# First loads, function table and idle products of a mixture-of-experts and attention kernel, and the place of one split

## Chip, core and metric

The kernel runs on one core of one Trainium2 chip. The metric is the device time of one execution in microseconds; lower is better. The engines are TensorE (PE, matrix products), VectorE (DVE), ScalarE (ACT), GpSimd (POOL) and SyncE (SP), which here issues every DMA transfer. Each engine has its own instruction queue, run in order; the queues meet only at semaphores.

## What is computed

Two layers in sequence on x of 8 x 512 x 256. The first picks one of eight experts for each of the 8 batches; the second is a transformer block with 16 heads of 16, a bias of 8 x 16 x 512 x 512 (134 MB, the main traffic) and an adaptive norm fed by an embedding of a time step.

```python
# layer 0, b = one of 8 batches, its expert read from itok_B_0_7
h = gelu(x[b] @ Wi[e] + bi[e])              # 512x256 @ 256x1024
y = layernorm(h @ Wo[e] + bo[e] + x[b]) * gamma[e] + beta[e]
# layer 1
emb = silu(sin_emb(timestep)) @ W_ada + b_ada          # one row per batch
scale, shift = split(emb)
x2 = layernorm(y) * (1 + scale) + shift
q, k, v = x2 @ Wq + bq, x2 @ Wk + bk, x2 @ Wv + bv     # 16 heads of 16
p = softmax(where(mask, -inf, q @ k.T / 4 + attention_bias))
x3 = x2 + (p @ v) @ Wo + bo
out = x3 + gelu2((layernorm(x3) * g2 + beta2) @ W1 + b1) @ W2 + b2
```

## The kernel before

Three stages follow each other: the first (to about 257 us) does layer 0 and q, k, v for all 8 batches; the second is the attention; the third the rest of layer 1. Only the beginning of the first stage is touched.

**Split products.** f32 matrices are multiplied as three products of rounded halves: for a matrix a, its high half is a copy to fp32r and its low half is a minus that copy; `mm3` (L606) issues high x high, low x high and high x low. So each operand has to be split before it is used: ScalarE makes the high half (`copy`, L827), then VectorE (`low`, L1054) or GpSimd (`low`, L1375) subtracts.

**First stage, batch i.** TensorE does eight tiles `hidden(i, m)`: six products of 512 columns each (two of K by three), into one of four banks psH; tile m waits until the low half of tile m-4 is out (`v_hTl`). ScalarE's `hidden` applies Gelu in place (L864) and copies the high half hTh; VectorE's `hidden` subtracts the low half hTl from the same bank. Then TensorE does four tiles `down(i, t)`, each of eight terms m of three products of 256 columns; term m waits for the low half of hidden tile m. For batch 0 it also waits for all of the second weights wo: VectorE splits pieces 0 and 2 (`v_wo0`), GpSimd pieces 1 and 3 (`g_wol`), each behind ScalarE's copy of that piece (`a_woh`). After `down(0, 3)` comes `embedding()` (L671), which needs a chain on VectorE, ScalarE (Sin, Exp, each with a function table) and VectorE again; then the hidden tiles of batch 1.

**VectorE in batch 0.** `embedding()` is a generator of short steps on tiles of 128 x 8, each of which waits for the one before (`step`). After every low half one part of it runs: four steps (L1092 to L1095, behind the wait `d_c` for time step and frequencies), three (L1097 to L1099), four (L1101 to L1104), three (L1107 to L1109), three (L1111 to L1113), four, three, and three more, the last of which waits for the small weights (`d_w`).

**GpSimd in batch 0.** In this order: the first weights' pieces 1 and 3, `split_wo(0)` (two pieces of wo), `add_bo(0)` (writes t_xb, L1404), then for batch 1 `split_xt(1)` (t_xTl) and `split_wi(1)` (t_wil). The last two wait only for ScalarE's copies, and these for the transfers and for the eighth hidden tile of TensorE. ScalarE's order is: x of batch 0, four slices of the first weights, hidden tiles, and behind the eighth x and weights of batch 1, the embedding's three functions, the small weights.

**SyncE.** `sync_program` issues all loads by `load` (L274), in program order; a wait in it holds all that stands behind. Before, the order is: identity, expert index, x of batch 0 (transposed, t_xt), time step and frequencies; value read of the index (it needs the index load); four slices of the expert's first weights t_wi_f, its bias, second weights t_wo_f, x, three rows for the norm (broadcast); wait for the step load; small weights and biases of layer 1 (eight loads, `d_w`); seven value reads (L315); then x, rows and bias of batch 1, and t_xt, t_wi_f, t_wo_f of batch 1.

Of the kernel before, what the change touches and what calls it, by code (L numbers as in the profile page):

```python
# [11 lines left out]
ACT = mybir.ActivationFunctionType  # L12
AX = mybir.AxisListType

B, S, D, I, H, HD = 8, 512, 256, 1024, 16, 16
NT = S // 128
NK = D // 128
# [46 lines left out]
def kpn(a):  # L64
    return a.rearrange("(k p) n -> p k n", p=128)
# [46 lines left out]
def program(nc, x, x_t, itok, tstep, bias, mask, Wi, bi, Wo0, bo0, gam, bet, Wada, bada, Wq, bq, Wk, bk, Wv, bv,  # L112
            Wo, bo, W1, b1, W2, b2, g2, be2, ident, freqs, out):
    with ExitStack() as ctx:
# [23 lines left out]
        d_id, d_it, d_c, d_w, d_xt, d_wi, d_wo, d_v, d_ss, d_ssb = (sem(f"d_{n}") for n in ("id", "it", "c", "w", "xt", "wi", "wo", "v", "ss", "ssb"))  # L138
        d_wi0 = [sem(f"d_wi0{i}") for i in range(4)]
# [11 lines left out]
        v_var1, v_var2, v_var3, g_pw, g_rs1, g_rs2, g_rs3 = (sem(n) for n in ("v_var1", "v_var2", "v_var3", "g_pw", "g_rs1", "g_rs2", "g_rs3"))  # L151
# [11 lines left out]
        idf = sbuf(base, "idf", [128, 128])  # L163
        idb = sbuf(base, "idb", [128, 128], BF16)
        half = sbuf(base, "half", [128, NT])
# [3 lines left out]
        with ExitStack() as st:  # L169
            psH = [psum(st, f"psH{i}", [128, 512]) for i in range(NH)]  # L170
            psO = psum(st, "psO", [128, NT, D])
            psQ = [psum(st, f"psQ{i}", [128, 512]) for i in range(2)]
            wi_f, wo_f = sbuf(st, "wi_f", [128, NK, I]), sbuf(st, "wo_f", [128, NM, D])
# [6 lines left out]
            itk = sbuf(st, "itk", [1, B], I32)  # L180
            tsb = sbuf(st, "tsb", [128, B], I32)
            frq = sbuf(st, "frq", [128, 1])
            em = sbuf(st, "em", [128, 8, 2 * B])
# [7 lines left out]
            bqk = sbuf(st, "bqk", [128, 2, NK])  # L191
# [78 lines left out]
        def sync_program(e):  # L270
            P = Port(e)

            def load(signal, dst, src):
                e.dma_start(dst, src).then_inc(signal, 16)  # L274


            load(d_id, idf[:, :], ident)
            load(d_it, itk[:, :], itok.rearrange("(a b) -> a b", a=1))
            load(d_xt, xt[:, :, :], kpn(x_t[0]))
            load(d_c, tsb[:, :], tstep.rearrange("(a b) -> a b", a=1).broadcast_to([128, B]))  # L280
            load(d_c, frq[:, :], freqs)
            P.wait_ge(d_it, 16)
            expert = {0: e.value_load(itk[0:1, 0:1], min_val=0, max_val=7)}

            def ix(b):
                return bass.ds(expert[b], 1)

            def load_bi(b):
                load(d_bi[b % 2], bis[b % 2][:, :], bi[ix(b), :, :].rearrange("e p m -> (e p) m"))

            def load_small(b):
                for n, a in enumerate((bo0, gam, bet)):
                    load(d_s[b % 2], ob[b % 2][:, n, :], a[ix(b), :].broadcast_to([128, D]))

            def load_x(b):
                load(d_x[b % 2], xs[b % 2][:, :, :], rows(x[b]))

            for i in range(4):
                sl = slice(i * I // 4, (i + 1) * I // 4)
                load(d_wi0[i], wi_f[:, :, sl], Wi[ix(0), :, sl].rearrange("e (k p) i -> p (e k) i", p=128))  # L300
            load_bi(0)
            load(d_wo, wo_f[:, :, :], Wo0[ix(0), :, :].rearrange("e (m p) n -> p (e m) n", p=128))
            load_x(0)
            load_small(0)
            P.wait_ge(d_c, 32)
            load(d_w, wad[:, :, :], kpn(Wada))
            load(d_w, bad, bada.rearrange("(a n) -> a n", a=1).broadcast_to([B, 2 * D]))
            load(d_w, bqk[:, 0, :], bq)
            load(d_w, bqk[:, 1, :], bk)
            load(d_w, bvb[:, :], bv.rearrange("(a n) -> a n", a=1).broadcast_to([128, D]))  # L310
            load(d_w, wstage["q"][:, 0:NK, :], kpn(Wq))
            load(d_w, wstage["k"][:, 0:NK, :], kpn(Wk))
            load(d_w, wstage["v"][:, 0:NK, :], kpn(Wv))
            for b in range(1, B):
                expert[b] = e.value_load(itk[0:1, b:b + 1], min_val=0, max_val=7)  # L315
            load_x(1)
            load_small(1)
            load_bi(1)

            def next_xt(b):  # L320
                if b < B:
                    if b == 1:
                        P.wait_ge(v_xT0, 1)
                    P.wait_ge(g_xTl, b - 1)
                    load(d_xt, xt[:, :, :], kpn(x_t[b]))

            def next_wi(b):
                if b < B:
                    P.wait_ge(v_wi0, 2)
                    P.wait_ge(g_wil, b + 1)  # L330
                    load(d_wi, wi_f[:, :, :], Wi[ix(b), :, :].rearrange("e (k p) i -> p (e k) i", p=128))

            def next_wo(b):
                if b < B:
                    P.wait_ge(v_wo0, 2)
                    P.wait_ge(g_wol, b + 1)
                    load(d_wo, wo_f[:, :, :], Wo0[ix(b), :, :].rearrange("e (m p) n -> p (e m) n", p=128))

            def next_x(b):
                if b < B:  # L340
                    P.wait_ge(g_xb, b - 1)
                    load_x(b)
# [33 lines left out]
            def store_x2(b):  # L376
                P.wait_ge(v_x2, b + 1)
                load(d_x2[b % 2], sc_x2[b], x2[b % 2][:, :, :])

            next_xt(1)  # L380
            next_wi(1)
            next_wo(1)
            next_x(2)
            next_bi(2)
            next_xt(2)
# [209 lines left out]
        def tensor_program(e):  # L595
# [78 lines left out]
            def first_stage():  # L674
                for i in range(B):
                    for m in range(NM):
                        hidden(i, m)
                        if m == 3 and i >= 2:
                            turn_x2(i - 2)
                    if i >= 2:  # L680
                        drain(qkv(i - 2))
                    for t in range(NT):
                        if i == B - 1 and t == NT - 1:
                            turn_x2(B - 2)
                        down(i, t)
                    if i == 0:
                        embedding()
# [88 lines left out]
            def down2(b, t):  # L776
# [4 lines left out]
                mm3(psO2[:, t, :], [([z[:, m, ts] for z in fT], [w[:, m, :] for w in wl["2"]]) for m in range(NM)], p_dn,  # L781
                    each=[(v_fTl, 8 * b + m + 1) for m in range(NM)])

            first_stage()
            P.wait_ge(v_hTl, 8 * B)
            at = 0
# [36 lines left out]
        def scalar_program(e):  # L823
# [79 lines left out]
            def first_stage():  # L903
                split_xt(0)
                split_wi(0)
                for i in range(B):
                    for m in range(NM):
                        hidden(i, m)
                        if m == 3 and i >= 2:
                            turn_x2(i - 2)  # L910
                        if m == 0 and i == 0:
                            split_wo0()
                    steps = qkv(i - 2) if i >= 2 else iter(())
                    for n in range(7):
                        advance(steps, 1)
                        if n == 3 and i + 1 < B:
                            split_xt(i + 1)
                            split_wi(i + 1)
                    if i == 0:
                        embedding()  # L920
                        split_small()
# [74 lines left out]
            def up(b, m):  # L996
# [7 lines left out]
                P.wait_ge(p_dn, NT * b)  # L1004
                copy(fT[0][:, m, :], f[:, :], a_fTh)

            first_stage()
            for t in range(NT):
                read_mask(0, t)
# [32 lines left out]
        def vector_program(e):  # L1042
# [153 lines left out]
            def first_stage():  # L1196
                P.wait_ge(a_xTh, 1)
                low(xT[1][:, :, :], xt[:, :, :], xT[0][:, :, :], v_xT0)
                for i in (0, 2):
                    sl = slice(i * I // 4, (i + 1) * I // 4)  # L1200
                    P.wait_ge(a_wih, i + 1)
                    low(wi_s[1][:, :, sl], wi_f[:, :, sl], wi_s[0][:, :, sl], v_wi0)
                e.memset(v17[:, :, :, HD:VW], 1.0).then_inc(v_one, 1)
                for i in range(B):
                    side = norms(i - 1) if i else embedding()
                    advance(side, 1 if i else 0)
                    for m in range(NM):
                        hidden(i, m)
                        if m == 3 and i >= 2:
                            turn_x2(i - 2)  # L1210
                        if i == B - 1:
                            advance(side, SIDE_END[m])
                        else:
                            advance(side, 1 if i == 0 else SIDE_A[0] if m > 3 else 0)
                        if m == 0:
                            split_wo(i)
                    steps = qkv(i - 2) if i >= 2 else iter(())
                    for n in range(6):
                        advance(steps, 1)
                        advance(side, 3 if i else 0)  # L1220
                    advance(steps, 1)
                    for t in range(NT):
                        advance(side, SIDE_A[1] if i else t % 2)
                        if i == 0 and t == 1:
                            split_small()
                    drain(side)
# [376 lines left out]
```

## Time and profile before

| what | us |
|---|---|
| median of 3 runs (1047.84 to 1049.8) | 1048.68 |
| the profiled execution, whole | 1049.58 |
| its span in the trace | 1047.8 |
| PE busy | 989.4 (94%) |
| DVE busy | 812.4 (78%) |
| ACT busy | 772.8 (74%) |
| POOL busy | 657.5 (63%) |
| PE idle at the start, until the first low half of the weights | 8.8 |
| PE idle in the first 110 us for low halves of hidden tiles | 3.6 in 3 waits |

The busy shares are averages over three stages with different limits. A timeline row gives start and duration of an instruction, or of several alike with their count (x4). A product's record is longer than the distance to the next, since products are pipelined: the pace is read from starts. The value in brackets is the idle time of the engine just before, and what ended it.

### The profile page before, as it was taken

What the parts mean: (1) busy time and instruction counts of PE and PEld (TensorE: products, weight loads), DVE (VectorE), ACT (ScalarE), POOL (GpSimd) and SP (SyncE); (2) the same over time, 40 slices, a digit from 0 to 9 for tenths busy, and PEclk for the clock granted to TensorE, in tenths of its full rate; (3) what the DMA queues carried; (4) which work ended last, traced back from release to release, by engine and by line L of the source; (5) the groups of instructions that cost most, each with busy time, mean ns of one, the idle gap of its engine ahead of it and who ended that gap; (6) DMA issues with size and microseconds to landing.
All of it is one profiled execution on the core that took longest, in us unless ns stands there. A gap on an engine that the chain in (4) does not pass through costs nothing.

```text
span 1047.8 us, 19216 instructions
## 1 busy us (share of the span) xinstructions
PE 989.4 (94%) x6678; PEld 738.0 (70%) x6744; DVE 812.4 (78%) x1934; ACT 772.8 (74%) x1283; POOL 657.5 (63%) x349
## 2 busy tenths in 40 slices
PE   5999999999899999999998999999998799999998
PEld 4889988898565555555555555565665599888897
DVE  5599999997878988788886888888887465655563
ACT  6755576555799999899997999999998344444444
POOL 3566766763357788778976798777876654444210
PEclk9999999999999999999999999999999899999999
DMA  8748688879989999999989999999999543221001
GB/s 228 267 153 275 230 294 282 311 261 359 349 335 421 362 391 362 381 366 351 364 326 338 342 333 376 366 356 367 318 338 254 102 109 82 81 83 41 21 22 41
DMA packets 107858, 278.63 MB, mean 266 GB/s; under 512 B 13026, under 2 KB 69090, under 8 KB 87154
## 3 DMA queue, kind: packets, MB, share of 16 engines
q1 hardware_dynamic: 107762, 277.40, 75.1%
q8 instruction: 55, 0.90, 0.3%
q14 instruction: 41, 0.34, 0.1%
HBM read 222.03 MB, written 55.33 MB: 265 GB/s over the span
## 4 chain that ended last, share of the span: by engine, by line
PE 55%; ACT 21%; DMA 9%; POOL 5%; DVE 5%; issue 4%; SPq 2%; DVEq 0%; ACTq 0%; POOLq 0%
PE psO L606 15%; PE psH L606 15%; ACT t_bt L937 11%; DMA t_bt<-in_fside_Bx16xSxS 8%; PE psT L722 8%; ACT t_pt L827 6%; PE psQ L606 4%; PE psS L711 4%; PE psV L735 3%; POOL t_bt L1452 3%; PE psA L606 2%; SPq L274 2%; PE psS L709 1%; ACT t_mb L959 1%; DVE t_y L1076 1%
## 5 line engine op out<-in xcount | busy, mean ns | idle before, releaser
L1452 POOL TENSOR_TENSOR t_bt<-t_bt,t_mb 128x1024 f32<-128x1024 f32 x182 | 384.5, 2145 | 115.1 <-DMA t_bt<-in_fside_Bx16xSxS 115.1
L1254 DVE CUSTOM_DVE_ANT_0 t_bt<-psS,t_bt 128x512 f32<-128x512 f32 x512 | 338.7, 686 | 85.1 <-PE psS L711 45.7
L937 ACT ACTIVATE t_bt<-t_bt,t_nm 128x512 f32<-128x512 f32 x512 | 358.4, 737 | 19.2 <-DVE t_nm L1254 18.9
L722 PE MATMUL psT<-t_idf,t_bt 128*128 128x128 f32 x2048 | 311.3, 275 | 10.5 <-ACT t_bt L937 8.9
L722 PEld LDWEIGHTS psT<-t_idf,t_bt 128*128 128x128 f32 x2048 | 251.3, 141 | 80.0 <-ACT t_bt L937 27.8
L827 ACT ACTIVATE t_pt<-psT 128x512 f32<-128x512 f32 x317 | 192.6, 608 | 16.8 <-PE psT L722 16.6
L711 PE MATMUL psS<-t_ks,t_qs 128*128 128x512 bf16 x482 | 184.2, 382 | 13.9 <-DVE t_nm L1254 9.0
L735 PE MATMUL psV<-t_pt,t_vs 128*17 128x512 f32 x1024 | 135.0, 601 | 0.0
L1264 DVE COPY t_pt<-psT 128x512 f32<-128x512 f32 x195 | 133.7, 686 | 1.3 <-PE psT L722 1.3
L711 PEld LDWEIGHTS psS<-t_ks,t_qs 128*128 128x128 bf16 x512 | 50.0, 98 | 91.0 <-DVE t_nm L1254 70.8
L864 ACT ACTIVATE psH<-psH,t_bi 128x512 f32<-128x512 f32 x64 | 42.3, 662 | 69.2 <-PE psH L606 66.3
L1054 DVE TENSOR_TENSOR t_chTl<-t_chf,t_chTh 128x512 fp32r<-128x512 f32 x64 | 53.3, 836 | 29.7 <-ACT t_chTh L827 29.7
L606 PE MATMUL psO<-t_cw2h,t_chTh 128*128 128x256 f32 x256 | 72.9, 285 | 0.0
L606 PE MATMUL psO<-t_woh,t_hTh 128*128 128x256 f32 x256 | 72.5, 283 | 0.0
L606 PE MATMUL psO<-t_woh,t_hTl 128*128 128x256 f32 x256 | 72.5, 283 | 0.0
L606 PE MATMUL psO<-t_wol,t_hTh 128*128 128x256 f32 x256 | 72.5, 283 | 0.0
L606 PE MATMUL psO<-t_cw2h,t_chTl 128*128 128x256 f32 x256 | 72.4, 283 | 0.0
L606 PE MATMUL psO<-t_cw2l,t_chTh 128*128 128x256 f32 x256 | 72.3, 283 | 0.0
L1002 ACT ACTIVATE t_chf<-psH,t_b1c 128x512 f32<-128x512 f32 x64 | 43.7, 683 | 29.7 <-PE psH L606 27.4
L606 PE MATMUL psH<-t_xTh,t_wih 128*128 128x512 f32 x128 | 52.4, 409 | 12.7 <-DVE t_wil L1054 8.8
L827 ACT ACTIVATE t_lTh<-psX 128x512 fp32r<-128x512 f32 x16 | 8.7, 595 | 73.9 <-PE psX L759 73.9
L1375 POOL TENSOR_TENSOR t_wol<-t_wo_f,t_woh 128x2048 fp32r<-128x2048 f32 (+1 forms) x9 | 35.5, 3952 | 37.1 <-DVE t_woh L1157 34.0
(174 smaller groups left out, 1933.9 us busy)
## 6 DMA issues: line engine op xcount, KB each, us to landing
t_bt<-in_fside_Bx16xSxS SPq DMA_DIRECT2D x128, 1024.0 KB, 7.8
sc_qk<-t_parts SPq DMA_DIRECT2D x64, 384.0 KB, 6.4
t_qs<-sc_qk SPq DMA_DIRECT2D x16, 1024.0 KB, 8.0
t_ks<-sc_qk SPq DMA_DIRECT2D x16, 1024.0 KB, 10.5
t_wo_f<-in_L_cond_Wo SPq DMA_DIRECT2D x8, 1024.0 KB, 6.2
sc_qk<-t_parts SPq DMA_DIRECT2D x32, 256.0 KB, 8.4
sc_c<-t_cv SPq DMA_DIRECT2D x32, 256.0 KB
t_wi_f<-in_L_cond_Wi SPq DMA_DIRECT2D x7, 1024.0 KB, 8.7
```

Of the source, the lines that this page charges most:

```text
L606: ins = e.matmul(dst, lh[a], rh[c], start=n == 0, stop=n == last)
L711: e.matmul(s, qs[g % 2][:, h % 8, t * 128:(t + 1) * 128], ks[g % 2][:, h % 8, :], start=on_pool(u), stop=True).then_inc(p_sc, 1)
L722: ins = e.transpose(psT[turned_bank(n)][:, kk, :], bt[u % NB][:, t, kk * 128:(kk + 1) * 128], idf[:, :])
L735: ins = e.matmul(psV[32 * g:32 * g + VW, :], vs[b % 2][:, kk, u % H, :], pt[u % NP][:, kk, :], start=kk == 0, stop=kk == NT - 1)
L827: e.activation(dst, src, ACT.Copy).then_inc(signal, 1)
L864: e.activation(f[:, :], f[:, :], ACT.Gelu, bias=bis[b % 2][:, m:m + 1]).then_inc(a_gelu, 1)
L937: e.activation(p, p, ACT.Exp, bias=nm[:, n % NR:n % NR + 1], scale=-1.0).then_inc(a_exp, 1)
L1002: e.activation(f[:, :], psH2[m % 2][:, :], ACT.Gelu_apprx_sigmoid, bias=b1c[:, m:m + 1]).then_inc(a_gel2, 1)
L1054: e.tensor_tensor(dst, src, high.bitcast(F32), ALU.subtract).then_inc(signal, 1)
L1254: e.tensor_tensor_reduce(bt[u % NB][:, t, :], s, bt[u % NB][:, t, :], -1.0, 3.0e38, ALU.add, ALU.min, nm[:, n % NR:n % NR + 1]).then_inc(v ...
L1264: e.tensor_copy(pt[u % NP][:, :, t * 128:(t + 1) * 128], psT[turned_bank(n)][:, :, :]).then_inc(v_ev, 1)
L1452: e.tensor_tensor(bt[u % NB][:, hs, :], bt[u % NB][:, hs, :], mb[b % 2][:, hs, :], ALU.add).then_inc(g_M, 1)
```

## The change

The loads at the start get another order: index, t_xt, identity; after the value read and the loads for batch 0 come the time step and frequencies, x, then t_xt of batch 1, the three rows of batch 0, t_wi_f of batch 1, the small weights, bias and t_wo_f of batch 1, its x and rows, and last six value reads. Before its first tile TensorE multiplies the identity by itself 14 times into a bank that is overwritten later. ScalarE runs one Gelu on a small constant tile before its first copy. On ScalarE and VectorE the split of the second weights of batch 0 moves from behind hidden tile 0 to behind hidden tile 3. The `next_...` and `store_...` helpers stand earlier in the file, unchanged.

```diff
-            load(d_id, idf[:, :], ident)
             load(d_it, itk[:, :], itok.rearrange("(a b) -> a b", a=1))
             load(d_xt, xt[:, :, :], kpn(x_t[0]))
-            load(d_c, tsb[:, :], tstep.rearrange("(a b) -> a b", a=1).broadcast_to([128, B]))
-            load(d_c, frq[:, :], freqs)
+            load(d_id, idf[:, :], ident)
             P.wait_ge(d_it, 16)
             expert = {0: e.value_load(itk[0:1, 0:1], min_val=0, max_val=7)}
...
+            def next_xt(b):
+                if b < B:
+                    if b == 1:
+                        P.wait_ge(v_xT0, 1)
+                    P.wait_ge(g_xTl, b - 1)
+                    load(d_xt, xt[:, :, :], kpn(x_t[b]))
+
+            def next_wi(b):
+                if b < B:
+                    P.wait_ge(v_wi0, 2)
+                    P.wait_ge(g_wil, b + 1)
+                    load(d_wi, wi_f[:, :, :], Wi[ix(b), :, :].rearrange("e (k p) i -> p (e k) i", p=128))
...
             load_bi(0)
             load(d_wo, wo_f[:, :, :], Wo0[ix(0), :, :].rearrange("e (m p) n -> p (e m) n", p=128))
+            load(d_c, tsb[:, :], tstep.rearrange("(a b) -> a b", a=1).broadcast_to([128, B]))
+            load(d_c, frq[:, :], freqs)
             load_x(0)
+            next_xt(1)
             load_small(0)
+
+            expert[1] = e.value_load(itk[0:1, 1:2], min_val=0, max_val=7)
+            next_wi(1)
             P.wait_ge(d_c, 32)
             load(d_w, wad[:, :, :], kpn(Wada))
...
             load(d_w, wstage["v"][:, 0:NK, :], kpn(Wv))
-            for b in range(1, B):
-                expert[b] = e.value_load(itk[0:1, b:b + 1], min_val=0, max_val=7)
+            load_bi(1)
+            next_wo(1)
             load_x(1)
             load_small(1)
-            load_bi(1)
...
-            next_xt(1)
-            next_wi(1)
-            next_wo(1)
+            for b in range(2, B):
+                expert[b] = e.value_load(itk[0:1, b:b + 1], min_val=0, max_val=7)
             next_x(2)
...
+            P.wait_ge(d_id, 16)
+            for _ in range(14):
+                e.matmul(psO[:, 0, 0:128], idf[:, :], idf[:, :], start=True, stop=True)
             first_stage()
...
-                        if m == 0 and i == 0:
+                        if m == 3 and i == 0:
                             split_wo0()
...
+            P.wait_ge(g_pw, 1)
+            e.activation(em[:, 7, 0:NT], half[:, :], ACT.Gelu)
             first_stage()
...
-                        if m == 0:
+                        if m == (0 if i else 3):
                             split_wo(i)
```

## Rows read from the trace of the kernel before

**Rows 1.** Windows: start:end, length, each engine's busy us, clock, DMA share, GB/s

```profile
8.80:11.90 3.10, 3.10 (x7) 2.49 (x8) 1.30 (x2) 2.29 (x4) 2.21 (x2) 1.00 0.94 294
...
21.90:25.40 3.50, 3.50 (x9) 2.73 (x10) 3.19 (x12) 0.94 (x3) 0.00 (x0) 0.52 1.08 224
...
80.00:100.00 20.00, 20.00 (x146) 19.00 (x146) 19.65 (x38) 7.64 (x9) 14.94 (x9) 1.00 0.84 277
```

**Rows 2.** Timeline of TensorE: start, us, line, out<-in, form, [idle before <-releaser]

```profile
26.32 0.27 PE L606 MATMUL psO<-t_woh,t_hTh 128*128 128x256 f32 x1
...
39.06 1.88 PE L671 MATMUL psQ<-t_qr,t_em 128*8 128x512 f32 x4 [1.08 <-DVE t_em L1125]
40.87 0.50 PE L606 MATMUL psH<-t_xTh,t_wih 128*128 128x512 f32 x1
...
70.30 1.09 PE L642 MATMUL psQ<-t_idf,t_x 128*128 128x128 f32 x8 [0.73 <-DVE t_x L1076]
```

**Rows 3.** Chain that ended last, in order of time: start, us, what

```profile
23.29 8.58 DMA t_wi_f<-in_L_cond_Wi
...
40.94 11.12 PE psH L606 x48
```

**Rows 4.** Timeline of VectorE, same columns

```profile
14.33 0.17 DVE L1093 TENSOR_SCALAR t_em<-t_em 128x8 f32<-128x8 f32 x1
...
14.95 2.40 DVE L1054 TENSOR_TENSOR t_wol<-t_wo_f,t_woh 128x512 fp32r<-128x512 f32 x2
17.45 0.69 DVE L1054 TENSOR_TENSOR t_hTl<-psH,t_hTh 128x512 fp32r<-128x512 f32 x1
...
18.52 2.30 DVE L1098 TENSOR_TENSOR t_em<-t_em 128x8 f32<-128x8 f32 x1
...
36.89 1.62 DVE L1123 TENSOR_SCALAR t_em<-t_em 128x16 f32<-128x16 f32 x1 [7.82 <-ACT t_em L899]
...
56.69 8.16 DVE L1076 SCALAR_TENSOR_TENSOR t_y<-t_y,t_rs,t_ob 128x256 f32<-128x256 f32 x4
```

**Rows 5.** Timeline of GpSimd, same columns

```profile
15.28 3.19 POOL L1375 TENSOR_TENSOR t_wol<-t_wo_f,t_woh 128x512 fp32r<-128x512 f32 x2 [3.03 <-ACT t_woh L827]
18.43 2.37 POOL L1404 TENSOR_TENSOR t_xb<-t_x,t_ob 128x1024 f32<-128x1024 f32 x1
...
33.88 4.60 POOL L1375 TENSOR_TENSOR t_wil<-t_wi_f,t_wih 128x2048 fp32r<-128x2048 f32 x1 [1.06 <-ACT t_wih L827]
...
56.64 2.39 POOL L1375 TENSOR_TENSOR t_xTl<-t_xt,t_xTh 128x1024 fp32r<-128x1024 f32 x1
58.99 4.79 POOL L1375 TENSOR_TENSOR t_wil<-t_wi_f,t_wih 128x2048 fp32r<-128x2048 f32 x1
```

**Rows 6.** Timeline of SyncE, which issues all transfers, same columns

```profile
1.19 0.30 SPq L274 DMA_DIRECT2D t_itk<-in_itok_B  x1
...
1.99 0.46 SPq L274 DMA_DIRECT2D t_tsb<-in_itok_B  x1
```

**Rows 7.** Transfers up to 60 us: engine, op, count, size, us to landing

```profile
t_idf<-ident SPq DMA_DIRECT2D x1, 64.0 KB, 1.9
...
t_tsb<-in_itok_B SPq DMA_DIRECT2D x1, 4.0 KB, 3.4
```

**Rows 8.** Timeline of ScalarE, same columns

```profile
5.42 1.06 ACT L827 ACTIVATE t_xTh<-t_xt 128x1024 fp32r<-128x1024 f32 x1 [3.41 <-DMA t_xt<-in_x_t]
...
10.91 1.28 ACT L864 ACT_TABLE_LOAD   x1
...
14.05 2.20 ACT L827 ACTIVATE t_woh<-t_wo_f 128x512 fp32r<-128x512 f32 x4 [0.55 <-DMA t_wo_f<-in_L_cond_Wo]
...
17.31 0.66 ACT L864 ACTIVATE psH<-psH,t_bi 128x512 f32<-128x512 f32 x1
...
18.49 0.66 ACT L864 ACTIVATE psH<-psH,t_bi 128x512 f32<-128x512 f32 x1
...
29.27 1.06 ACT L827 ACTIVATE t_xTh<-t_xt 128x1024 fp32r<-128x1024 f32 x1 [1.46 <-DMA t_xt<-in_x_t]
```

More of the change, by code:

```diff
@@ L296, in load_x @@
                 load(d_x[b % 2], xs[b % 2][:, :, :], rows(x[b]))
[L298 to L313, printed above, removed]
-            for b in range(1, B):
-                expert[b] = e.value_load(itk[0:1, b:b + 1], min_val=0, max_val=7)
-            load_x(1)
-            load_small(1)
-            load_bi(1)
             def next_xt(b):
@@ L378, in store_x2 @@
                 load(d_x2[b % 2], sc_x2[b], x2[b % 2][:, :, :])
+            for i in range(4):
+                sl = slice(i * I // 4, (i + 1) * I // 4)
+                load(d_wi0[i], wi_f[:, :, sl], Wi[ix(0), :, sl].rearrange("e (k p) i -> p (e k) i", p=128))
+            load_bi(0)
+            load(d_wo, wo_f[:, :, :], Wo0[ix(0), :, :].rearrange("e (m p) n -> p (e m) n", p=128))
+            load(d_c, tsb[:, :], tstep.rearrange("(a b) -> a b", a=1).broadcast_to([128, B]))
+            load(d_c, frq[:, :], freqs)
+            load_x(0)
             next_xt(1)
+            load_small(0)
+            expert[1] = e.value_load(itk[0:1, 1:2], min_val=0, max_val=7)
             next_wi(1)
+            P.wait_ge(d_c, 32)
+            load(d_w, wad[:, :, :], kpn(Wada))
+            load(d_w, bad, bada.rearrange("(a n) -> a n", a=1).broadcast_to([B, 2 * D]))
+            load(d_w, bqk[:, 0, :], bq)
+            load(d_w, bqk[:, 1, :], bk)
+            load(d_w, bvb[:, :], bv.rearrange("(a n) -> a n", a=1).broadcast_to([128, D]))
+            load(d_w, wstage["q"][:, 0:NK, :], kpn(Wq))
+            load(d_w, wstage["k"][:, 0:NK, :], kpn(Wk))
+            load(d_w, wstage["v"][:, 0:NK, :], kpn(Wv))
+            load_bi(1)
             next_wo(1)
+            load_x(1)
+            load_small(1)
+            for b in range(2, B):
+                expert[b] = e.value_load(itk[0:1, b:b + 1], min_val=0, max_val=7)
             next_x(2)
```

## Prediction

> **What bounds the kernel now.** I read the windows view of the first 260 us first. In the seven windows from 80 to 230 us TensorE is busy for the whole time (one of them stands in [rows 1]): in the first stage it is the bound, each batch costs the same, and the attention behind it starts from events, not at fixed times. So whatever this change does is settled before the second batch's first hidden tile, which starts at 40.87 us [rows 2], and a shift of that start should reach the end one for one. Call that start H1. Next the TensorE timeline and the chain of waits up to H1: first product at 8.80, with 3.10 us for its first seven (0.44 each) [rows 1] where the steady pace is 11.12/48 = 0.23 [rows 3]; a second slow stretch at 21.90 with a granted clock of 0.52 [rows 1], after gaps in which the engine waited for low halves of the hidden tiles; the down products from 26.32 to 37.98, 96 at 0.12; then a wait of 1.08 for the embedding, its product of four records in 1.88, and H1 [rows 2]. The visible losses are these: about 17.5 us for 48 hidden products that take 11.1 warm (6.4 lost), 1.1 of waiting, and the late start. That is what could be won. Last I read ScalarE, VectorE and GpSimd beside each other, because the low half of each hidden tile passes through VectorE between tiny embedding steps.
>
> **What decides: two engines that exclude each other.** VectorE ops that read only SBUF stop while a GpSimd op runs. The 128x8 add of line 1098 took 2.30 us, ending with GpSimd's 2.37 us add of t_xb; the 128x16 tensor_scalar of line 1123 took 1.62, ending with t_wil; with GpSimd idle such a step takes 0.17, as at 14.33 [rows 4, 5]. A low half of a hidden tile reads one PSUM operand and took its normal 0.69 at 17.45 while t_wol ran on GpSimd [rows 4, 5]. Where both engines have a queue they alternate: the four t_y ops from 56.69 took 8.16, beside t_xTl (2.39) and t_wil (4.79, where it took 4.60 alone at 33.88) run back to back: one slipped in between the two, the others ran in the 1.07 after 63.78 [rows 4, 5]. The two t_wol ops of VectorE at 14.95 (2.40) and GpSimd's two at 15.28 (3.19) interleave in the same way [rows 4, 5].
>
> **The change, part by part.**
> *Start.* The index load goes from second place (1.19) to first, one issue earlier, so the value read and the four weight slices come 0.46 us earlier [rows 6]: first data for TensorE at 8.3 instead of 8.8.
> *Idle products.* The identity now stands behind the 512 KB of t_xt. The tiny step load in the same position lands 3.4 us after its issue at 1.99, that is at 5.4, just as t_xt lands (5.42) [rows 6, 7]. So I put the identity with t_xt, at 5.0; the bound below is its old flight of 1.9 from its new issue at 1.53, 3.4 [rows 6, 7]. Two f32 products of the embedding show as four records [rows 2], so 14 make 28 records, 512 columns there and 128 here. One of 128 columns costs 0.12 (a quarter of the embedding's 0.47 for 512) to 0.14 (1.09/8 of the transposes at 70.30) at full clock, double at half [rows 2]. With 3.1 us at half clock first [rows 1]: some 11 records there, 17 at 0.13 behind, 5.2 us in all. They end at 10.3, later than the data (8.3). Bounds: 8.7 with the early identity, 12.8 if the clock does not rise. The first real tile then runs warm, 10.3 to 11.9 where it was 8.8 to 11.7: this part alone wins nothing at tile 0 and 1.2 us over tile 1.
> The Trainium skill, DMA: Bandwidth & Descriptors, section "Anatomy of one DMA", gives about 2.0 us of fixed cost for a transfer; by that as an estimate the identity would land at 3.5 and the idle products end near 8.8, and the same ledger as below would give +3 us at H1 instead of +6. The step load's 3.4 us speaks against it here.
> *Function table.* The load of 1.28 at 10.91 [rows 8] goes to the start, where ScalarE idles until 5.42 [rows 8]. It ended only 0.5 after tile 0's end, so it is worth up to 0.5, and nothing once tile 0 ends at 11.9.
> *Hidden tiles.* Warm, eight tiles at 1.39 (11.12/8): 10.3 to 21.4 [rows 3]. ScalarE needs 1.18 a tile (17.31 to 18.49) [rows 8], so it keeps pace up to tile 3. No bank wait is left as long as VectorE keeps up.
> *Split of the second weights, behind tile 3.* ScalarE's four copies (2.1 us) [rows 8] now run from 17.1 to 19.2; tiles 4 to 7 start at 19.2, 20.4, 21.6, 22.8, and tile 7's high half is out at 24.1. Before, the last tile left TensorE near 26.5 [rows 2], so its high half was out near 27.8.
> *Earlier loads of the next batch.* t_xt of batch 1 is issued at about 8.3, and t_wi_f at about 12.4, when the last slice is split (before: 23.29, just behind t_xt [rows 3]); even with its old flight of 8.58 [rows 3] it lands at 21. So ScalarE splits x of batch 1 at 24.0 (before: 29.27, when the load landed [rows 8]) and the weights right behind, and GpSimd gets t_xTl (2.4) at 25.1 and t_wil (4.6) [rows 5] directly after. Before, t_xTl could start only at 30.3 (29.27 and the 1.06 of the split) and t_wil at 33.88 [rows 5, 8], after the last low half, and they held up only line 1123. This is the turn: the late transfers were what kept GpSimd out of VectorE's way.
> *The ledger of VectorE and GpSimd.* VectorE: low half 3 at 17.3, three steps from 17.9. GpSimd's t_wol at 18.3 (second copy out, as 15.28 stands 1.23 after 14.05 [rows 5, 8]) to 19.6; third step 19.6; GpSimd's second t_wol 19.8 to 21.1; VectorE's first t_wol 21.1 to 21.7; GpSimd's t_xb 21.7 to 24.0; VectorE's second t_wol 24.0 to 24.6; low half 4 at 24.7; then three steps, held by t_xTl (25.1 to 27.5). One passes, t_wil takes 27.7 to 32.3, the other two pass after it. Low half 5 is at 32.7, four steps, 6 at 34.1, three steps, 7 at 35.3 to 35.9.
> *TensorE at the down products.* It may begin at 24.8, does five of eight terms of tile 0, and stands until 33.3; tile 0 is done at 36.3 to 36.6. Three more tiles are 72 x 0.12 = 8.6 [rows 2]: 45.2. After some 5 us idle the clock will be at half again, but 3.1 us of it pass inside the waits for terms 5 to 7; if it counts from later, up to 1.5 more. The embedding's result is ready at 40, so its product follows at once, 1.85 (the 1.08 wait is gone). H1 = 47.0, against 40.87: +6.1.
> *Parts at nothing.* The small weights and biases are issued 4 us later, after the wait for the step load, which now lies behind 1 MB of second weights, and land near 25; their reader, ScalarE, comes after 38. t_wo_f of batch 1 is issued at about 25 (before: just behind 23.29), x and the rows for the norm behind it; their readers come 3.6 and more after H1. Six value reads of 0.55 move behind them and delay only loads of batch 2, with 10 us of room. The idle products write a bank that the down product restarts. SP's new waits on the first splits (12.3) hold only these loads. Should one of these covers fail, it would add to the delay.
>
> **From the ledger to the time.** The same ledger, worked for the kernel before, gives 40.94 for H1 (measured 40.87), so its rules are good for some tenths. For the change I moved the unknowns: idle products ending at 8.3 to 10.9, the step load landing at 13 to 16.5, weights of batch 1 at 19 to 24. H1 moves by +1.7 to +8.4, four fifths of it between +2.7 and +6.6, since a VectorE held earlier also slows ScalarE and so GpSimd's t_xTl. I take +5.5. The profiled execution was 1049.58 (span 1047.8), 0.9 above the median of 1048.68: 1055.1 for it, 1054.2 for the median.
>
> **Rivals.**
> (A) *The exclusion does not bite in the new order*, because the short steps find room before each GpSimd op or their waits are shorter than t_y's. Then ScalarE sets the pace: last low half at 25.0, down products over at 34.2, H1 at 35.9: -5.1, 1043.6. For it: all visible losses go away as intended. Against it: lines 1098, 1123 and 1076, all held to the end of a GpSimd op. Chance 0.20.
> (B) *VectorE, once it has the port, keeps it for its whole queue.* Then only t_xTl and t_xb hold it, t_wil waits, and H1 moves by 0 to +2: 1049.9. Against it: the 8.16 us of t_y, which that order would not give. Chance 0.08.
> (C) *The change does not do what it says with the loads*: x and weights of batch 1 still land at 28 and 31 because the queue is full of broadcasts. Then the last low half is out at 29.5, and H1 at 40.3: -0.6, 1048.1. It needs transfers of over 16 us where this one took 8.58 [rows 3]. Chance 0.06.
>
> **Chances and range.** Forecast 0.66 (all of it above +1.7 us). What a measurement of this kernel can tell from no change is 0.2%, 2.1 us. Some 0.02 of the forecast's cases fall inside it, and B and C nearly whole: same 0.15, faster 0.20, slower 0.65. The range must leave out no more than 2 in 10: A is left out, B and C are in: 1048.0 to 1057.0; the likeliest case's own is 1050.4 to 1057.
>
> **What would show it.** Right: H1 at 43 to 48; GpSimd's t_xTl before low half 6; a short embedding step of VectorE of 4 to 5 us, ending with t_wil; TensorE waiting 4 us or more for t_hTl inside the first down tile. Identity landing near 5, 28 idle records, first hidden product near 10.3 and warm. Wrong: low half 7 before 27, or embedding steps at 0.17 while t_xTl runs; then A, and the time is near 1044. If H1 is later and the time is not, the shift is taken up downstream, against the steady windows.

## The result and the profile after

| what | before | after |
|---|---|---|
| median of 20 runs (us) | 1047.78 | 1052.16 |
| lowest and highest | 1043.83, 1052.87 | 1045.72, 1055.77 |
| the profiled execution, whole | 1049.58 | 1050.19 |
| its span in the trace | 1047.8 | 1048.4 |

The ratio of after to before is 1.0042, with a 95% interval of 1.0028 to 1.0057: 4.4 us slower (2.9 to 6.0). The two profiled executions lie only 0.6 apart, since that of before was 1.8 above its median and that of after 2.0 below its own. So the spans must not be subtracted. What can be compared is the order of events in the first 110 us.

The line numbers of after are 8 higher on VectorE, GpSimd and in the low halves (L1062 for L1054, L1383 for L1375), and 1 higher on TensorE.

The chain that ended last, stretch by stretch, in the columns of [rows 3]. First after:

```profile
1.59 3.50 DMA t_idf<-ident
5.13 5.93 PE psO L788 x28
...
20.34 4.48 DVE t_wol L1062 x2
...
25.73 2.38 DVE t_em L1121
28.14 0.69 DVE t_hTl L1062
28.83 3.74 DVE t_em L1125
...
34.29 0.70 DVE t_hTl L1062
35.03 10.46 PE psO L607 x75
45.50 1.81 PE psQ L672 x4
47.31 11.12 PE psH L607 x48
...
92.87 11.52 PE psO L607 x96
```

H1 is the row of 48 hidden products: 47.31, where [rows 3] has 40.94, so it moved by 6.4. Ahead of it stands VectorE from 15 to 35 us, which before was on this chain only with the last three embedding steps (36.89 to 39.02), behind the late load and ScalarE; and in it two embedding steps on 128x8 elements, of 2.38 and 3.74 us. A later point shows that nothing is given back within the first stage. The second batch's 96 down products, in after the last row above, stand in before at:

```profile
86.50 11.52 PE psO L606 x96
```

This is 6.37 earlier, and VectorE's first op on the attention's bias also stood 6.38 later in after (265.12 against 258.74).

VectorE of after, the timeline's columns as in [rows 4]:

```profile
24.74 0.68 DVE L1062 TENSOR_TENSOR t_hTl<-psH,t_hTh 128x512 fp32r<-128x512 f32 x1
25.34 0.15 DVE L1119 SCALAR_TENSOR_TENSOR t_em<-t_em 128x8 f32<-128x8 f32 x1
25.53 0.17 DVE L1120 SCALAR_TENSOR_TENSOR t_em<-t_em 128x8 f32<-128x8 f32 x1
25.73 2.37 DVE L1121 SCALAR_TENSOR_TENSOR t_em<-t_em 128x8 f32<-128x8 f32 x1
28.14 0.69 DVE L1062 TENSOR_TENSOR t_hTl<-psH,t_hTh 128x512 fp32r<-128x512 f32 x1
28.75 3.83 DVE L1125 TENSOR_SCALAR t_em<-t_em 128x8 f32<-128x8 f32 x1
...
33.09 0.69 DVE L1062 TENSOR_TENSOR t_hTl<-psH,t_hTh 128x512 fp32r<-128x512 f32 x1
...
34.29 0.69 DVE L1062 TENSOR_TENSOR t_hTl<-psH,t_hTh 128x512 fp32r<-128x512 f32 x1
```

GpSimd of after in the same stretch, which [rows 5] had at 33.88 for the weights:

```profile
18.98 2.54 POOL L1383 TENSOR_TENSOR t_wol<-t_wo_f,t_woh 128x512 fp32r<-128x512 f32 x2 [7.43 <-ACT t_woh L832]
21.48 2.79 POOL L1412 TENSOR_TENSOR t_xb<-t_x,t_ob 128x1024 f32<-128x1024 f32 x1
25.69 2.39 POOL L1383 TENSOR_TENSOR t_xTl<-t_xt,t_xTh 128x1024 fp32r<-128x1024 f32 x1 [1.42 <-ACT t_xTh L832]
28.04 4.51 POOL L1383 TENSOR_TENSOR t_wil<-t_wi_f,t_wih 128x2048 fp32r<-128x2048 f32 x1
```

Read the ends side by side. The step at 25.73 ends at 28.10 and t_xTl at 28.08; the step at 28.75 ends at 32.58 and t_wil at 32.55. The steps around them take 0.15 to 0.17, and the low halves, which read PSUM, 0.68 to 0.69, also the one at 28.14, which ran while t_wil did. So GpSimd did not slow the low halves, but the tiny steps queued between them.

Who waits for that is on TensorE:

```profile
24.87 0.58 PE L607 MATMUL psO<-t_woh,t_hTh 128*128 128x256 f32 x1 [2.90 <-DVE t_wol L1062]
...
28.88 0.58 PE L607 MATMUL psO<-t_woh,t_hTh 128*128 128x256 f32 x1 [0.44 <-DVE t_hTl L1062]
...
33.84 0.58 PE L607 MATMUL psO<-t_woh,t_hTh 128*128 128x256 f32 x1 [3.94 <-DVE t_hTl L1062]
...
35.03 0.58 PE L607 MATMUL psO<-t_woh,t_hTh 128*128 128x256 f32 x1 [0.19 <-DVE t_hTl L1062]
```

The hidden products, eight tiles in 11.0 us at the pace 0.23, are over at 21.8; what they won is lost in four waits of 7.5 us together. The first, 2.90, is for the low halves of the second weights, which VectorE had done only at 24.8, since its two ops took turns with GpSimd's (4.48 us for both); the other three, 4.6, are for low halves of hidden tiles. A second price of the waits is the clock. Windows of after, the columns as in [rows 1]:

```profile
24.80:29.00 4.20, 3.69 (x16) 3.40 (x16) 4.10 (x7) 3.90 (x3) 3.31 (x2) 0.50 0.71 218
29.00:33.40 4.40, 0.89 (x3) 0.59 (x3) 4.30 (x5) 0.00 (x0) 3.54 (x1) 0.50 0.81 256
35.00:38.00 3.00, 2.96 (x14) 2.97 (x15) 1.09 (x7) 2.65 (x4) 0.00 (x0) 0.54 1.08 353
38.00:45.50 7.50, 7.50 (x64) 7.37 (x63) 1.89 (x3) 2.12 (x5) 0.00 (x0) 1.00 0.24 94
```

The granted clock is 0.50, its level of 1.2 GHz, from the first down product to the last wait, and still 0.54 in the first 3 us of unbroken work behind it. The 75 products from 35.03 take 10.46, where 75 at 0.12 are 9.0.

### The profile page after: what moved, and what is told of

Its sections match the earlier page's. It is cut to its first block, busy times and chain, and to the rows that moved or that the text cites. A ratio compares the mean times of both kernels' runs of the same rounds, so it can differ in the third digit from the quotient of the medians.

```text
span 1048.4 us, 19272 instructions
## 1 busy us (share of the span) xinstructions
PE 992.6 (95%) x6706; PEld 742.7 (71%) x6772; DVE 817.1 (78%) x1934; ACT 772.0 (74%) x1283; POOL 657.4 (63%) x349
## 4 chain that ended last, share of the span: by engine, by line
PE 54%; ACT 20%; DMA 9%; DVE 6%; POOL 6%; issue 3%; SPq 2%; DVEq 0%; ACTq 0%; POOLq 0%
PE psO L607 16%; PE psH L607 15%; ACT t_bt L942 11%; DMA t_bt<-in_fside_Bx16xSxS 8%; PE psT L723 7%; ACT t_pt L832 6%; PE psQ L607 4%; POOL t_bt L1460 4%; PE psS L712 4%; PE psV L736 3%; SPq L274 2%; PE psA L607 2%; PE psS L710 1%; DVE t_y L1084 1%; ACT t_mb L964 1%
## 5 line engine op out<-in xcount | busy, mean ns | idle before, releaser
L607 PE MATMUL psO<-t_woh,t_hTh 128*128 128x256 f32 x256 | 74.7, 292 | 7.5 <-DVE t_hTl L1062 4.6
L1062 DVE TENSOR_TENSOR t_chTl<-t_chf,t_chTh 128x512 fp32r<-128x512 f32 x64 | 53.1, 831 | 30.5 <-ACT t_chTh L832 30.5
L1383 POOL TENSOR_TENSOR t_wol<-t_wo_f,t_woh 128x2048 fp32r<-128x2048 f32 (+1 forms) x9 | 34.9, 3881 | 53.8 <-DVE t_woh L1165 46.3
L607 PEld LDWEIGHTS psO<-t_woh,t_hTh 128*128 128x128 f32 x256 | 50.0, 195 | 8.8 <-DVE t_hTl L1062 5.5
## 6 DMA issues: line engine op xcount, KB each, us to landing
t_ks<-sc_qk SPq DMA_DIRECT2D x16, 1024.0 KB, 10.9
```

The source lines that it names most:

```text
L607: ins = e.matmul(dst, lh[a], rh[c], start=n == 0, stop=n == last)
L1062: e.tensor_tensor(dst, src, high.bitcast(F32), ALU.subtract).then_inc(signal, 1)
```

## The experiments

The theory: the earlier loads let GpSimd's t_xTl and t_wil start at 25 to 28 instead of 30 to 34, and there they hold embedding steps that stand in VectorE's queue ahead of low halves 5 to 7. The rivals: the split behind tile 3 by itself (late second weights), or the idle products, or the queue of transfers. All kernels compute the whole reference; times of before are those of runs on the same chip.

**GpSimd told to wait.** Everything of the change stays, but t_xTl of batch 1 may start only once all eight low halves are out.

```diff
             def split_xt(b):
+                P.wait_ge(v_hTl, 8 if b == 1 else 0)
                 P.wait_ge(a_xTh, b + 1)
```

> The changed kernel with one wait more: GpSimd starts t_xTl of batch 1 only when the last low half of batch 0 is out. Theory (GpSimd's t_xTl and t_wil of batch 1 keep the embedding steps between low halves 5 and 7 waiting): the last low half comes at about 29.6 us instead of 34.3, the down products end at about 39 instead of 45.5, and H1 (first hidden product of batch 1) is 40.5 to 44.3, the upper end if the embedding step L1131 now meets t_wil; time 3 to 6.5 us below the changed kernel's (ratio to before 0.9995 to 1.003). Rival (the loss comes from the split behind tile 3 and the idle products, which only start everything later): the last low half stays near 34, and since GpSimd now starts its 7 us later still, H1 is 47 or later and the ratio 1.004 or more.

Measured: ratio 0.9988 (0.9969 to 1.0008), H1 at 40.24. VectorE and GpSimd:

```profile
28.44 0.69 DVE L1062 TENSOR_TENSOR t_hTl<-psH,t_hTh 128x512 fp32r<-128x512 f32 x1
...
33.45 2.89 DVE L1131 TENSOR_SCALAR t_em<-t_em 128x16 f32<-128x16 f32 x1 [1.62 <-ACT t_em L904]
```

```profile
29.21 2.40 POOL L1383 TENSOR_TENSOR t_xTl<-t_xt,t_xTh 128x1024 fp32r<-128x1024 f32 x1 [6.13 <-DVE t_hTl L1062]
31.57 4.74 POOL L1383 TENSOR_TENSOR t_wil<-t_wi_f,t_wih 128x2048 fp32r<-128x2048 f32 x1
```

Low half 4 comes at 24.76, as in after (24.74), but the last one at 28.44 instead of 34.29, with GpSimd's work made 3.5 us later. The exclusion is still there: L1131 takes 2.89 and ends with t_wil. But by then TensorE has all it needs for its down products (29.19 to 38.43), and the wait costs nothing. With one wait added the loss is gone and the theory stands. H1 is 0.3 below the expected range, and 0.7 below that of before, which is too little to be told from nothing (see the last experiment).

**The loads of the next batch late again.** The other way to keep GpSimd out: the loads of batch 1 stand last again, as before. The step load stays where after has it, behind the second weights, and all else is as in after.

```diff
             load_x(0)
-            next_xt(1)
             load_small(0)
-
-            expert[1] = e.value_load(itk[0:1, 1:2], min_val=0, max_val=7)
-            next_wi(1)
...
+            for b in range(1, B):
+                expert[b] = e.value_load(itk[0:1, b:b + 1], min_val=0, max_val=7)
             load_x(1)
             load_small(1)
...
+            load_bi(1)
+            next_xt(1)
+            next_wi(1)
+            next_wo(1)
```

> The changed kernel with the loads of t_xt and t_wi_f of batch 1 back behind the small weights and the value reads. Theory: they land near 30 to 35 us, so t_xTl and t_wil on GpSimd come after the last low half, which is out at 29.6 instead of 34.3; the down products end near 39; H1 is then set by t_wil, 43 to 46, because these loads are now later than in the kernel before (the small weights wait for the step load behind the second weights). Ratio to before 1.001 to 1.004. Rival (the late low halves do not come from GpSimd's work for batch 1): the last low half stays at 34 and H1 is over 47.

Measured: ratio 1.0041 (1.0019 to 1.0063). Low half 4 comes at 24.85 and the last one at 28.52, so the cause of the late low halves is confirmed a second time, from the side of the transfers. Yet the time is that of after, by another wait. The chain:

```profile
25.25 9.73 DMA t_wi_f<-in_L_cond_Wi
35.00 1.91 ACT t_wih L830
36.93 1.28 ACT L900
...
42.10 3.25 PE psQ L670 x4
45.35 11.14 PE psH L605 x48
```

The weights' load, issued at 25.25 behind the small weights and seven value reads, lands at 35; ScalarE splits it ahead of the embedding's functions, TensorE waits 3.6 us for the embedding, and the four records of its product take 3.25 instead of 1.81. The expectation named t_wil as what sets H1; it does so only in part, by one embedding step (L1129, 1.56) that it held to its end at 41.5, and the rest is the late load. H1 is 45.35. So the place of the loads is not free in either direction: early, they release GpSimd too soon; late, they hold ScalarE.

**The split alone put back** behind hidden tile 0, early loads kept.

```diff
-                        if m == 3 and i == 0:
+                        if m == 0 and i == 0:
                             split_wo0()
...
-                        if m == (0 if i else 3):
+                        if m == 0:
                             split_wo(i)
```

> The changed kernel with the split of the second weights back behind hidden tile 0. Theory (the low halves are late because VectorE reaches them with its steps still undone when GpSimd's work for batch 1 arrives): with the split at tile 0 GpSimd's t_wol and t_xb are over before low half 4, VectorE has caught up, and the last low half is out near 30, down products end near 39.5, H1 near 41 instead of 47.2; ratio to before about 1.000. Rival (the early loads alone decide, wherever the split stands): H1 stays at 46 or more, ratio 1.004 or more.

Measured: ratio 0.9969 (0.9949 to 0.9989), H1 at 39.77, 1.2 below before, where the expectation had 41 and a ratio of about 1.000. VectorE and GpSimd:

```profile
27.96 0.69 DVE L1062 TENSOR_TENSOR t_hTl<-psH,t_hTh 128x512 fp32r<-128x512 f32 x1
...
30.26 4.54 DVE L1125 TENSOR_SCALAR t_em<-t_em 128x8 f32<-128x8 f32 x1
```

```profile
27.81 2.39 POOL L1383 TENSOR_TENSOR t_xTl<-t_xt,t_xTh 128x1024 fp32r<-128x1024 f32 x1 [5.49 <-ACT t_xTh L832]
30.16 4.62 POOL L1383 TENSOR_TENSOR t_wil<-t_wi_f,t_wih 128x2048 fp32r<-128x2048 f32 x1
```

The longest hold of all, 4.54, costs nothing here, because it falls on a step behind the last low half. Why GpSimd comes just late enough is seen on ScalarE:

```profile
21.80 0.66 ACT L869 ACTIVATE psH<-psH,t_bi 128x512 f32<-128x512 f32 x1 [1.64 <-PE psH L607]
...
26.68 1.05 ACT L832 ACTIVATE t_xTh<-t_xt 128x1024 fp32r<-128x1024 f32 x1
```

With the split behind tile 0, VectorE is late with low halves 1 to 3, so TensorE waits for a bank at tile 5 (1.9), ScalarE waits with it, and the fourth to the seventh low half keep step with the high halves; x of the next batch is split at 26.68 and t_xTl starts beside the last low half. In after, VectorE's delay comes behind low half 3, when all four banks are free: TensorE and ScalarE run through tiles 4 to 7, ScalarE reaches x at 24.57, and four low halves with their steps are still to come. So the early loads lose nothing without the late split. The late split without the early loads was not run alone: with late loads (above) it leaves the low halves in time, and the 4.3 us lost there come by the load. The held low halves belong to the pair.

**The idle products taken away** from after.

```diff
-            P.wait_ge(d_id, 16)
-            for _ in range(14):
-                e.matmul(psO[:, 0, 0:128], idf[:, :], idf[:, :], start=True, stop=True)
             first_stage()
```

> The changed kernel without the 14 idle products. Theory: they are neither the loss nor a gain while the low halves wait for GpSimd: first hidden product at 8.4 and slow, last low half at 34 to 36, H1 at 46 to 47.5, ratio 1.003 to 1.006 as for the changed kernel. Rival (the idle products delay the first tile from 8.4 to 10.8 and all behind it by the same): H1 2 us lower, 45, ratio 1.002.

Measured: ratio 1.0064 (1.0041 to 1.0087), H1 at 47.42 against 47.31. The ratio is just above the expected 1.003 to 1.006, but its interval holds that of after. The idle products neither win nor lose at H1 while VectorE holds the down products; there the step held by t_wil was L1117, 4.42 us, and TensorE's wait 5.0.

**Steps out of the way.** If steps between low halves are the price, the steps should run before GpSimd starts or after the last low half. Here the time step and frequencies are loaded ahead of the second weights, so the steps can begin before tile 0; none stands between low halves 3 and 7; and t_xTl waits until the steps behind the last one are done. The idle products are nine.

```diff
+            load(d_c, tsb[:, :], tstep.rearrange("(a b) -> a b", a=1).broadcast_to([128, B]))
+            load(d_c, frq[:, :], freqs)
             load_bi(0)
             load(d_wo, wo_f[:, :, :], Wo0[ix(0), :, :].rearrange("e (m p) n -> p (e m) n", p=128))
...
-                    advance(side, 1 if i else 0)
+                    advance(side, 1 if i else 2)
...
-                            advance(side, 1 if i == 0 else SIDE_A[0] if m > 3 else 0)
+                            advance(side, (1, 1, 1, 0, 0, 0, 0, 3)[m] if i == 0 else SIDE_A[0] if m > 3 else 0)
...
             def split_xt(b):
+                P.wait_ge(v_ang, 2 if b == 1 else 0)
```

> The changed kernel with the contention taken out: time step and frequencies loaded ahead of the second weights, the first seven embedding steps ahead of low half 0, ten more behind low halves 0 to 2, the last ten behind low half 7, and GpSimd waits for these before t_xTl of batch 1; 9 idle products instead of 14. Theory: last low half at 24 to 26, down products end at 33 to 35, H1 at 35.4 to 37.4, which is 3.5 to 5.5 below the kernel before; ratio 0.9945 to 0.997. Rival (ScalarE, TensorE's start or loads hold the beginning, not the exclusion of the two engines): H1 not below 40, ratio 1.000 or more.

Measured: ratio 0.9959 (0.9939 to 0.9979), faster than before and than after, and H1 is 0.8 below the expected 35.4 to 37.4. The chain:

```profile
20.31 0.56 ACT psH L869
...
22.71 0.70 DVE t_hTl L1062
...
23.46 9.25 PE psO L607 x75
32.70 1.86 PE psQ L672 x4
34.56 11.12 PE psH L607 x48
```

H1 is 34.56, which is 6.4 before that of before and 12.8 before that of after, with the same early loads and the same split behind tile 3. ScalarE, not VectorE, sets the pace up to the last low half, 22.71, and TensorE waits only 0.6 at the down products. The hold is not gone: L1131, at 28.52, takes 3.62 and ends with t_wil at 32.1, and the embedding is ready at 32.6, when the down products end too. So it costs nothing, but with no room left. This is what rival (A) would have given; it needed the steps moved, not only the loads.

**The same without its idle products.** 

> The kernel of e4_steps without its 9 idle products. There the start of the hidden tiles is on the path that sets H1. Theory: H1 at 35.5 to 36.5 instead of 34.5, so the warm start is worth 1 to 2 us: ratio to before 0.996 to 0.998 (e4_steps: 0.9959). Rival (ScalarE sets the pace from tile 0 on, a warm start gives nothing): H1 34.5, ratio as e4_steps.

Measured: ratio 0.9949 (0.9924 to 0.9973), H1 at 35.35. In these two executions the idle products are worth 0.8 at H1, less than the expected 1 to 2, and the ratio lies below the expected 0.996 to 0.998. Neither at H1 nor in the time can they be told from nothing.

**What a shift at H1 is worth at the end.** Before, with unread products behind the embedding: eleven, then 33 (the same edit with `range(33)`).

```diff
                         embedding()
+                        for _ in range(11):
+                            e.matmul(psQ[1][:, :], idf[:, :], wad[:, 0, :], start=True, stop=True)
```

> The kernel before with 11 f32 products of 512 columns more on TensorE, just before the hidden tiles of batch 1 (22 records of 0.455 us, 10.0 us, into a bank nobody reads then). It measures how a shift of H1 reaches the end. Theory of the prediction: one for one, +10 us, ratio 1.0095. Rival (part of a shift is given back in the attention stage, as the profile of the changed kernel lets one think, with +6.4 at the end of the first stage and +0.6 at the end): clearly less, +5 to +8, ratio 1.005 to 1.0075.

> The kernel before with 33 f32 products of 512 columns ahead of the hidden tiles of batch 1: 66 records of 0.475 us, 31.3 us (the 11 of the run before took 10.45 and gave a ratio of 1.0104 for a shift of H1 of 12.4). One for one: H1 +31 to +33, ratio 1.030 to 1.032. If a fifth of a shift is given back later, as the five ratios so far would allow: ratio 1.024 to 1.026.

Measured: 1.0104 (1.0075 to 1.0133) and 1.0244 (1.0217 to 1.0270). Their chains, eleven first:

```profile
42.87 10.45 PE psQ L689 x22
53.32 10.93 PE psH L606 x48
```

```profile
40.70 28.52 PE psQ L689 x66
69.22 10.94 PE psH L606 x48
```

The shifts at H1 are 12.4 and 28.3; a record took 0.43 to 0.48. Of the 12.4, 10.45 are the products; the rest is that the embedding's product started 1.1 later and took 0.8 longer in that execution than in that of before. Up to this product the two kernels are the kernel before, and it ended at 42.87 and 40.70 in them, at 40.94 in before. So H1 of one execution is good to some 2 us: the shifts of 4 and more below are clear, those of 0.7 and 1.2 are not. All pairs together, H1 from one execution each, the time from the ratio:

| kernel | H1 | shift at H1 | time against before |
|---|---|---|---|
| steps moved | 34.56 | -6.4 | -4.3 (-6.4 to -2.2) |
| steps moved, no idle products | 35.35 | -5.6 | -5.3 (-8.0 to -2.8) |
| split behind tile 0 | 39.77 | -1.2 | -3.2 (-5.3 to -1.2) |
| GpSimd waits | 40.24 | -0.7 | -1.3 (-3.2 to +0.8) |
| loads late | 45.35 | +4.4 | +4.3 (+2.0 to +6.6) |
| after | 47.31 | +6.4 | +4.4 (+2.9 to +6.0) |
| no idle products | 47.42 | +6.5 | +6.7 (+4.3 to +9.1) |
| 11 products | 53.32 | +12.4 | +10.9 (+7.8 to +13.9) |
| 33 products | 69.22 | +28.3 | +25.6 (+22.7 to +28.3) |

A line through the origin, weighted by the intervals, has the slope 0.88, plus or minus 0.08 if the rows were independent, which those of one chip are not quite, and without the uncertainty of H1. The 33 products alone give 0.90 (0.80 to 1.00); the 10.9 of the 11 products is one for one against the 10.45 that they took. So a shift of H1 reaches the end at some nine tenths, and one for one is not excluded.

## Why the prediction was right, point by point

- **The turn.** Right: t_xTl at 25.69 (forecast 25.1), t_wil at 28.04 (27.7), a step of 3.83 that ends with t_wil, TensorE's waits for t_hTl in the first down tile 4.6 in three (over 4 forecast). The kernel in which GpSimd is told to wait changes nothing but GpSimd's start and confirms the cause; that with the late loads confirms it from the side of the transfers. The Trainium skill, SBUF — State Buffer, section "SBUF: two separate sides", has the same rule for a VectorE op with two SBUF inputs or in a two-port mode: whichever of the two engines starts first gets the shared ports for the whole instruction, the other blocks. The trace agrees: the step at 25.73 has two SBUF inputs, t_xTl started at 25.69, and 25.73 + 2.37 = 28.10 stands against t_xTl's end at 28.08.
- **The ledger in detail.** Two details differ. At low half 4 (24.74; forecast 24.7) two of three steps slipped through before t_xTl began, so low half 5 ran at 28.14, not 32.7, and t_wil caught a step behind it. Low half 7 came at 34.29 (35.3), and tile 0 was done at 35.84 (36.3 to 36.6). The clock took that back: the 72 products behind tile 0 took 45.50 - 35.84 = 9.7, not 8.6, since it stayed at half for almost 3 us after the last wait, a loss that I had set only as a bound. Two misses of about 1 us with opposite signs left H1 at 47.31, forecast 47.0. That it came so close is luck; the order of events is not.
- **The start.** The identity landed at 5.1 (forecast 5.0), 3.5 us after its issue, and 28 records followed. The estimate by the Trainium skill, DMA: Bandwidth & Descriptors, section "Anatomy of one DMA", was 1.6 too early; that section describes transfers issued by GpSimd, and here SyncE issues them all. The records ended at 10.81, forecast 10.3. Both terms of that step were off: a record costs 0.21 at half clock (19 between 5.93 and 9.98) and 0.11 at full, less than my 0.24 to 0.28 and 0.12 to 0.14, but the pace doubled only 5.3 us after the first record, not 3.1. Without idle products the first hidden product stood at 8.2, as forecast for the data (8.3).
- **Function table, loads, covers.** The table is loaded at 0.73 and none at 10.91. But before, too, a table was loaded at 0.73, for ScalarE's first copy, so one load of two is gone rather than moved; what that is worth, forecast as nothing, no run tells. Right: ScalarE split x of batch 1 at 24.57 without a wait for a transfer (24.0), the weights of batch 1 had landed at 21.8 (21), and the small weights, issued 3.4 us later than before, held nobody. Rival (C) is out with that. Rival (B) is out too: t_wil started at 28.04, directly behind t_xTl and with VectorE's queue full, and the step at 28.75 waited for its end. Rival (A) is out for this order of steps, and is what the version with moved steps reaches.
- **From H1 to the time.** The time lay in the range, but this term was mis-sized. I took +5.5 of a possible +1.7 to +8.4 at H1 and carried it one for one: 1054.2. H1 moved by 6.4, and of that 4.4 (2.9 to 6.0) is seen at the end; the median is 1052.16. Of the 2.0 between the two times, 0.9 is the median of before (1048.68 of 3 runs, 1047.78 of 20), and 1.1 the size. The lower pick for H1 helped: with the 6.4 that was measured, the same sum gives 1055.1, 2.9 too high. The shift is whole at VectorE's first op on the attention's bias: from H1 to that op it is 217.6 to 217.8 us in all ten kernels. What may absorb a part of it lies behind. From that op to the start of the last copy out of psV, at the end of the attention, the five profiled executions with an H1 later than that of before have 566.2 to 569.6 us, and the other five 569.7 to 572.6. So on average some 3 us of a late start seem to be made up there, but not in proportion to the shift (566.2 in that of after, 567.9 in that of +28.3). These are single executions, and which wait gives the time back is open.

## What to carry to other kernels

Before a load is made earlier, ask which GpSimd op it releases, and which short SBUF-only steps of VectorE stand between results that TensorE waits for: a late transfer may be what keeps the two engines apart. If both improvements are wanted, move the short steps out of that stretch or hold the GpSimd op behind it; here this turned +0.4% into -0.4%. And judge a wait by what it holds: the 4.54 us step cost nothing behind the last low half, the 3.83 us step ahead of it cost TensorE a wait of 3.94 and part of its clock.

## What was unexpected of the hardware

- A small transfer on the same queue lands with the large ones ahead of it. In after the 64 KB identity took 3.5 us and landed at 5.1, just behind the 512 KB of x at 4.9 (1.9 in [rows 7], as the first in the queue). The 4 KB step load took 6.2 and the 0.5 KB of frequencies 7.0; they landed at 12.4 and 13.8, the second weights ahead of them at 13.1.
- ScalarE loads the next function's table before it waits for its operand. In after:

```profile
27.43 1.28 ACT L902 ACT_TABLE_LOAD   x1
35.30 0.21 ACT L902 ACTIVATE t_em<-t_em 128x16 f32<-128x16 f32 x1 [6.58 <-DVE t_em L1125]
```

- The granted clock is no guide in the first 10 us: it is printed as 1.00 for the whole block of idle products, while the pace of their records doubled at about 10.4 in after and at about 9.0 with GpSimd waiting, a kernel in which TensorE's program is the same. In before it is 1.00 as well for the first seven products, at 0.44 each [rows 1].
